# Moving the slot table, the shared expert's additions and the first head's second values in a fused layer on one Trainium2 core

## What is computed

```python
xn = _layernorm(x)
x = x + attn(xn) + ffn(xn)

# attn: gated delta rule, 16 key heads, 2 value heads for each
qkvz = xn @ W_qkvz;  ba = xn @ W_ba
q, k, v = silu(causal convolution of 4 taps over the tokens)
q, k = l2norm(q), l2norm(k)                    # over 128 entries
M = -tril((k*beta) @ k.T * decay, -1);  T = inverse(I - M)
for each chunk:                                # state runs along the chunks
    vn  = T @ (v*beta) - (T @ (k*beta*exp(g))) @ state
    out = (q*exp(g)) @ state + (q @ k.T * decay) @ vn
    state = state*exp(g_last) + (k*exp(g_last - g)).T @ vn
x = rmsnorm(core * silu(z)) @ W_out

# ffn: softmax attention of 16 heads, then 4 of 16 experts and a shared expert
hid  = xn + attention(rmsnorm(xn)) @ o_w
x2   = rmsnorm(hid);  top_w, top_i = top_k(softmax(x2 @ gate_w.T), 4)
routed = sum over the 4 of top_w * (silu(g)*u @ w2)     # g, u = x2 @ w1
shared = silu(sg)*su @ sh_down_w.T
return hid + routed + shared
```

## Time and profile before

| | |
|---|---|
| median of 3 runs | 1561.87 us (1560.09 to 1562.95) |
| the profiled execution | 1560.7 us, its span 1558.9 us |
| TensorE busy | 1521.3 us, 98% of the span |
| VectorE busy | 1104.9 us, 71% |
| ScalarE busy | 779.8 us, 50% |
| GpSimd busy | 442.8 us, 28% |
| mean granted TensorE clock | 0.991 of full speed |
| chain that ended last | 92% TensorE, 3% VectorE |

### The profile page before, as it was taken

The page is one execution under the profiler, slowest core; times in us unless marked ns, Lnnn a source line. Parts: engine busy times, 40 slices in busy tenths (PEclk is TensorE's granted clock), DMA queues, the critical chain, the costliest instruction groups (busy, mean ns, idle before and its releaser), DMA issues.

```text
span 1558.9 us, 29212 instructions
## 1 busy us (share of the span) xinstructions
PE 1521.3 (98%) x10946; PEld 1075.1 (69%) x10946; DVE 1104.9 (71%) x2452; ACT 779.8 (50%) x1680; POOL 442.8 (28%) x280
## 2 busy tenths in 40 slices
PE   6999999999998999899999999999999999999998
PEld 4666666766656775567767767767767668668767
DVE  5364444565376435498988988988888988988966
ACT  3444435344423334564664664664564565565552
POOL 1000000006033004243543543643541541541511
PEclk9999999999999999999999999999999999999999
DMA  4342443113234434314414314324323323223211
GB/s 134 98 149 95 155 144 100 62 61 123 76 108 127 120 107 116 91 33 106 106 34 106 92 49 105 89 54 104 68 60 90 68 62 85 68 66 86 61 20 35
DMA packets 225051, 136.88 MB, mean 88 GB/s; under 512 B 160976, under 2 KB 196304, under 8 KB 224912
## 3 DMA queue, kind: packets, MB, share of 16 engines
q1 hardware_dynamic: 221840, 126.62, 30.2%
q0 software_dynamic: 3072, 8.39, 1.8%
HBM read 94.85 MB, written 35.91 MB: 84 GB/s over the span
## 4 chain that ended last, share of the span: by engine, by line
PE 92%; DVE 3%; issue 1%; ACT 1%; DMA 1%; SPq 0%; POOL 0%; POOLq 0%; DVEq 0%; ACTq 0%
PE ps L953 7%; PE ps L814 7%; PE ps L575 7%; PE ps L835 7%; PE ps L670 4%; PE ps L600 4%; PE ps L1089 4%; PE ps L704 4%; PE ps L857 3%; PE ps L890 3%; PE ps L742 3%; PE ps L590 3%; PE ps L752 3%; PE ps L1112 3%; PE ps L867 3%; PE ps L889 3%
## 5 line engine op out<-in xcount | busy, mean ns | idle before, releaser
L1440 ACT ACTIVATE vs<-ps 128x256 f32<-128x256 f32 x128 | 49.2, 384 | 255.6 <-PE ps L857 251.2
L2389 POOL TENSOR_TENSOR qg<-qT,Ebc 128x1024 f32<-128x1024 f32 x32 | 74.7, 2357 | 353.8 <-PE ps L890 328.9
L1944 DVE SCALAR_TENSOR_TENSOR cv<-ps,cw,cv 128x1022 f32<-128x1022 f32 (+2 forms) x96 | 122.7, 1279 | 17.7 <-ACT cv L1380 13.8
L1955 DVE SCALAR_TENSOR_TENSOR cv<-ps,cw,cv 128x1022 f32<-128x1022 f32 (+2 forms) x96 | 122.6, 1277 | 4.0 <-ACT cv L1412 1.6
L835 PE MATMUL ps<-xnT,gz 128*128 128x512 f32 x256 | 122.3, 602 | 0.7 <-DVE cv L1944 0.6
L953 PE MATMUL ps<-wout,xT 128*128 128x256 f32 x480 | 121.4, 395 | 0.0
L575 PE MATMUL ps<-xrT,cv 128*128 128x512 f32 x256 | 117.8, 593 | 1.1 <-ACT xrT L1277 0.8
L814 PE MATMUL ps<-xnT,gv 128*128 128x512 f32 x256 | 117.6, 603 | 0.5
L2083 DVE SCALAR_TENSOR_TENSOR total<-ps,rr,total 128x256 f32<-128x256 f32 x240 | 111.6, 480 | 5.7
L1340 ACT ACTIVATE we<-ps,bias 128x128 f32<-128x128 f32 (+3 forms) x128 | 65.8, 526 | 98.2 <-DVE bias L1764 98.2
L1760 DVE TENSOR_TENSOR ps<-ps,causal_neg 128x128 f32<-128x128 f32 x128 | 37.3, 292 | 105.2 <-PE ps L600 105.2
(11 more groups left out here) (265 smaller groups left out, 3577.3 us busy)
## 6 DMA issues: line engine op xcount, KB each, us to landing
xs_dram<-zeros SPq DMA_DIRECT2D x16, 1024.0 KB, 7.6
dec<-grow_dram SPq DMA_DIRECT2D x32, 512.0 KB, 4.8
Ebc<-erow_dram SPq DMA_DIRECT2D x32, 512.0 KB, 5.1
cv<-in_wqk SPq DMA_DIRECT2D x16, 512.0 KB, 3.5
xn<-xs_dram SPq DMA_DIRECT2D x47, 128.0 KB, 2.1
ys_dram<-yg SPq DMA_DIRECT2D x47, 128.0 KB, 1.9
we<-in_we SPq DMA_DIRECT2D x16, 352.0 KB
cv<-in_wv SPq DMA_DIRECT2D x16, 256.0 KB, 3.6
```

Of the source, the lines that this page charges most:

```text
L1944: ins = stt(row, pair(bank)[:, :, 0:S - k], cw[:, f, i, TAPS - 1 - k:TAPS - k], row, ALU.mult, ALU.add)
L1955: ins = stt(row, pair(bank)[:, :, 0:S - k], cw[:, n, 2 + r, TAPS - 1 - k:TAPS - k], row, ALU.mult, ALU.add)
```

## The change

The same instructions are issued; only their order changes. On VectorE, `slots()` moves from behind the first two shared additions to a place ahead of `up_times_gate(5)`, and the first two shared additions move behind the first convolutions. On ScalarE, `silu_value(0, 1)` and `gate_silu(0, 0)` move ahead of the squares of head 1. On TensorE, `key_squares(1)` moves behind the second turned values and the second gates.

```diff
@@ TensorE, ahead of the loop over heads
             first_beside_64(0)
-            key_squares(1)
             turn_values(0, 1)
             for b in range(B):
                 project_gates(0, 1, b)
+            key_squares(1)
             second_beside_64_and_first_of_128(0)
@@ ScalarE, ahead of the loop over heads
             silu_query(1)
+            silu_value(0, 1)
+            gate_silu(0, 0)
             squares(1, 0)
             squares(1, 1)
             values(0, 0)
             values(0, 1)
-            gate_silu(0, 0)
             beside_64(0)
-            silu_value(0, 1)
             gate_silu(0, 1)
@@ VectorE, around the shared expert
             expert_starts()
+            slots()
             up_times_gate(5)
...
-            add_shared(0)
-            add_shared(1)
-            slots()
             dve.wait_ge(fl["d_k"], 16 * 2)
             convolve_keys(0, 1)
             convolve_keys(0, 0)
+            add_shared(0)
+            add_shared(1)
             add_shared(2)
             add_shared(3)
             answers()
```

## The result

| | before | changed |
|---|---|---|
| median | 1561.87 us | 1549.09 us (5 runs, 1547.74 to 1553.02) |
| profiled execution, its span | 1560.7, 1558.9 us | 1548.47, 1546.7 us |
| mean granted TensorE clock | 0.991 | 0.998 |

The ratio is 0.9926, with an interval of 0.9909 to 0.9944: 11.6 us less, between 8.7 and 14.2. The page's first part shows the same busy engines as before; what differs is TensorE, 1514.5 us and not 1521.3, though it issues the same instructions. The clock by slices of the span reads 9 tenths throughout on both pages, so it is too coarse to show where; the mean clock is 0.998 for 0.991.

The account below looks back on a forecast made before the run. TensorE, busy 539.65 of 540 us in the loop, was taken as the bound, with gains only in its gaps. 2.1 + 5.9 - 1.1 = 6.9 us off 1561.87 gave 1555.0 us, range 1551.8 to 1558.8.

Parts of the forecast that it names:

- part A: VectorE edit ahead of the expert tiles: first expert product sooner, 2.1 us gained, bounds 0.9 and 2.3.
- the table in VectorE's idle time: Ahead of the expert tiles: the table runs from 454.4 to 459.7 us, mostly while VectorE had idled.
- the convolutions from the keys' tap: On VectorE ahead of the tiles: convolutions wait for the keys' tap at 461.91 and run 461.95 to 469.66 us.
- the additions as the last to open the sums: Ahead of the tiles: four additions end at 472.1, after the squares at 471.9; TensorE starts at 472.15, not 474.43.
- row loads that bind: At the tiles' start: rows hold the second turned tile until 478.0; first expert product at 478.2, not 480.42.
- The second rival: Ahead of the tiles: held scatters delay the row loads, leaving a gain of 0.9 there and 1556.2 us; chance 0.08.
- Part B: ScalarE and TensorE edits ahead of the loop over heads: first recurrence product at 643.45, not 649.38, 5.9 us gained before clock loss.
- GpSimd not in the way: Ahead of the loop: GpSimd's decays allow the first recurrence product at 642.7; TensorE itself comes last, at 643.45.
- the clock: Ahead of the loop: a TensorE clock fall after new idle times costs 1.1 us, bounds 0 and 3.1.
- The first: Rival: clock falls in both places, costing 0.5 ahead of the tiles and 3.1 ahead of the loop; 1557.5 us, chance 0.20.
- The third: Rival ahead of the loop: late key sums set the pace, their path 4 us longer; 1558.9 us, chance 0.10.
- fourth: Rival ahead of the loop: key sums held 11 us behind the gates, kernel slower at 1565 us; chance 0.03.

Follow-up runs that it names:

- the groups with the stall: Three middle groups of runs, where the unchanged kernel before took 1574 to 1576 us and not 1559 to 1561.
- The second pair of traces: Unchanged repeats of the kernel before and the changed kernel; 1559.41 us and 1549.48 us, lines 742 to 1089 in 23.11 and 21.29 us.
- the three further moves: Changed kernel with two additions back ahead of the convolutions, key sums between the second gates' halves, head 1's decays earlier; 0.9959, 0.9949 and 0.9922 of before.
- The filled gap: Kernel before with its order, plus unread products in TensorE's gaps: five ahead of the first sums, three at tiles' end, three ahead of the second values; ratio 0.9978.
- B alone: Kernel before with only the ScalarE and TensorE edits ahead of the loop over heads; 1553.52 us, ratio 0.9964.
- either half of B: Kernel before with only the ScalarE edit of the first head, ratio 0.9994, or only the TensorE edit, ratio 1.0008.
- The half scatters: Changed kernel with 8 and not 16 scatters in the second batch, so another output; 1565.47 us, ratio 0.9943 to before.

## Why the prediction was right or wrong

**The direction, and part A.** Right in the shown traces; in the groups with the stall A was worth nothing that can be told, since the scatters' end opened the sums. The steps held one by one: the table in VectorE's idle time, the convolutions from the keys' tap, the additions as the last to open the sums, a gap of 2.97 (2.8 forecast), row loads that bind, line 1089 2.17 us sooner (2.1). The second pair of traces gives 1.8. The second rival did not come: one stretched scatter, as before.

**Part B.** Right in its mechanism, at each wait: 0.93 and 0.73 for 0.85 and 0.9, the wait of 1.45 gone, GpSimd not in the way, TensorE itself last. It measured 6.25 and not 5.9.

**The step that failed: the clock.** The forecast had 6.9 us, the shown traces differ by 12.2, and 5.3 are missing: 1.45 at part B and 3.9 elsewhere. At part B the prediction said: "I take 1.1, since I hold a short fall somewhat likelier than none." No fall came in that stretch in any trace that has both halves of B (ten, four of them with the three further moves). I had argued from the fall of before at 632.6, and read it as the work of 0.61 and 1 us of idle time. The filled gap shows the other reading: with the same 0.61 us ahead of the same sums, but the 3.62 us gap full, the clock stayed at full. B with its clock is 6.25 where I had 4.8, 1.45 of the miss: 1.1 by the clock and 0.35 in the rest of the sum. That the low clock of before was itself worth 2.0 of B's 6.25 us was in the sum, through the rows at half clock, but not told apart.

**The term that was missing.** I looked for low clock only where instructions moved, and put it at nothing elsewhere. The earlier trace rows has two low stretches; the trace had five, besides the span's last 1.2 us. One, near 414 us, is in the traces of both kernels. The two others, behind the tiles and in the last heads, are worth 2.51 and 1.36 us of the difference: 3.9 us, most of the miss. The fall in the last heads is not the order's: the second trace of before has none, and the second and fourth of the changed kernel have one, at 1504 us. Its 1.36 us were luck of the two executions. Behind the tiles it is open. Both traces of before have the fall (27.96 and 27.75 us) and none of the changed kernel has it (25.4 to 25.5). But B alone and either half of B have the program of before up to there, and were at full clock: with that program two of five traces fell, which speaks for chance. Against chance alone stands the mean clock over the timed executions, 0.997 for the changed kernel in two further groups and 0.992 and 0.991 for before, a difference that the known stretches don't fill; in the group with the stall it was only 0.992 for 0.990.

**The base.** The 3 runs gave 1561.87, and later ones centre at 1559.2. By the ratios the change is worth 9.5 us (7.5 to 11.7), 11.6 (8.7 to 14.2) and 14.0 (12.0 to 16.2) in the groups without the stall; the first and the last of these intervals do not meet, and why is open. I had put 1.8 us on the scatter of the median. Executions of one program spread over 7 us with their clock (1555.3 to 1562.44 in the 32 of the first group), so the low end should have lain deeper; a forecast of 8.2 without a fall, on a base of 1559, would have been 1551.

**The rivals.** The first, that the clock takes back, is the opposite of what came. The third and fourth, late key sums, did not come: the sums began 8.8 us ahead of line 857, where the forecast had 8.9. The sentence that nothing behind the loop's start waits on a fixed time was too strong: it held for this change to 0.3 us over 13 heads, but not for the three further moves.

## What to carry to other kernels

Read the granted clock over the whole span ahead of any sum, not only where instructions move: on this kernel, which TensorE fills to 98%, the gaps of 3.6 and 5.1 us cost their length and, in the products behind them, 2 us more, gaps of 0.9 and 0.7 us did not, and the same program differs by 7 us with the clock. Two edits on two engines that open one meeting point have to be costed together, since either alone only moves the wait. A gain ahead of a transfer is worth what the transfer lets through: check what the loads wait for before adding up the compute.

## What the runs showed of the hardware that I had not expected

In three groups of runs VectorE and ScalarE stood still for a while beside GpSimd's indirect scatters, though nothing recorded held it. It was 4.90 us ahead of the last two additions, 3.71 and 2.38 in others. Beside the first batch's scatters VectorE stood for 5.7 to 9.2 us and ScalarE for 8.9 to 11.2 in all twelve traces of these groups. The key projection, behind that, started at 464.6 to 474.6 us of the span there and at 456.4 to 457.8 in all other traces, so most of the 15 us lies ahead of it. In the other groups no trace shows any of it, and the kernels of the last group ran on the same chip as those of the second. The half scatters show that the second stall ends with the scatters and is tied to no place in the program; the first batch's stall, whose scatters were all issued, stayed at 5.7 us in that run. What the engines wait for is open. One could think of the supply of instructions behind the scatters, but nothing traced supports it: within the 4.90 and the 3.71 us every packet is of the scatters' own queue, and no packet of the two instruction queues came between the stall's start and VectorE's going on.

A 128x16 addition on VectorE beside GpSimd's 128x2048 addition took 4.5 to 4.6 us in every trace but the last one with the three moves. There it was done before GpSimd began and took 0.17; a cast of 128x32 beside GpSimd's addition took 3.95 us instead, for 0.18 in the changed kernel. In both cases VectorE went on when GpSimd's addition ended, to within 0.1 us. A scatter that began 0.2 to 0.3 us behind the start of a 1x752 instruction of the table took 1.56 and 1.51 us for 0.96. The Trainium skill (GPSIMD Engine Reference, Key points) has the two engines contend over shared SBUF interfaces; these rows agree.
